# Layer 2's attention: one PSUM copy on ScalarE, one block of row sums earlier, and another order of work on GpSimd

## The reference, cut to what matters

```python
xn = layernorm(x, g1)
q = xn @ Wq.T                                   # 16 heads of 64
k, v = split(xn @ Wkv.T)                        # one head of 64 each
q, k = l2norm(q * 16) * 4, l2norm(k) * 4
sim = where(causal, q @ k.T, -max)
attn = softmax(sim)
out = layernorm((attn @ v) @ Wout.T, g2)
x = x + out + (silu(xn @ w_gate) * (xn @ w_up)) @ w_down
```

## Time and profile before

| | before |
|---|---|
| median of 3 runs | 1240.59 (1240.56 to 1241.66) |
| the profiled execution's own time | 1239.02 |
| its span, first to last instruction | 1237.2 |
| granted PE clock, mean over the span | 0.98 |
| busy: PE | 1145.6 (93%) |
| busy: DVE | 921.7 (74%) |
| busy: ACT | 672.3 (54%) |
| busy: POOL | 490.6 (40%) |

### The profile page before, as it was taken

The page is one execution under the profiler, slowest core; times in us unless marked ns, Lnnn a source line. Parts: engine busy times, 40 slices in busy tenths (PEclk is TensorE's granted clock), DMA queues, the critical chain, the costliest instruction groups (busy, mean ns, idle before and its releaser), DMA issues.

```text
span 1237.2 us, 26393 instructions
## 1 busy us (share of the span) xinstructions
PE 1145.6 (93%) x8475; PEld 782.4 (63%) x8475; DVE 921.7 (74%) x2473; ACT 672.3 (54%) x1290; POOL 490.6 (40%) x691
## 2 busy tenths in 40 slices
PE   5999999999999998899399999999999999999996
PEld 3656666666666554799265857657576575765764
DVE  7888888888888897455456868668686686866755
ACT  2767676666676755355173552735527355273550
POOL 5122212121222311554364481744817448274450
PEclk8999999999999998899799999999999999999999
DMA  3311212020101000122011030210302103021020
GB/s 89 101 44 48 56 28 57 26 60 26 33 18 27 18 18 1 44 64 55 15 35 27 9 59 0 42 25 8 59 0 42 25 8 59 0 49 19 15 46 10
DMA packets 43718, 42.31 MB, mean 34 GB/s; under 512 B 7040, under 2 KB 36224, under 8 KB 43648
## 3 DMA queue, kind: packets, MB, share of 16 engines
q0 software_dynamic: 11008, 17.31, 8.0%
q1 hardware_dynamic: 32640, 24.15, 7.3%
HBM read 13.72 MB, written 6.75 MB: 17 GB/s over the span
## 4 chain that ended last, share of the span: by engine, by line
issue 19%; PE 11%; POOL 9%; DVE 7%; DMA 3%; ACT 1%; POOLq 0%; DVEq 0%; ACTq 0%
PE pair L496 4%; POOL q_len L1272 3%; DMA arena<-arena 3%; PE gather L496 2%; PE ring_d L496 2%; POOL arena L1231 2%; POOL arena L1313 2%; PE ring_a L496 1%; PE pair L500 1%; DVE q_len L1958 1%; DVE stats L1574 1%; POOL arena L1293 1%; DVE arena L2106 1%; DVE q_rn L1960 1%; ACT arena L1515 1%
## 5 line engine op out<-in xcount | busy, mean ns | idle before, releaser
L1378 ACT ACTIVATE arena<-ring_a 128x384 f32<-128x384 f32 (+1 forms) x512 | 253.6, 550 | 147.1 <-PE ring_a L496 146.9
L1126 POOL TENSOR_SCALAR_AFFINE_SELECT arena<-arena 128x512 f32<-128x512 f32 x128 | 82.4, 643 | 366.6 <-ACT arena L1378 366.4
L496 PE MATMUL ring_a<-q_max,rows 128*128 128x384 f32 (+1 forms) x512 | 197.2, 388 | 2.2 <-DVE q_max L1684 1.8
L1670 DVE CUSTOM_DVE_ANT_0 arena<-pair,arena 128x384 bf16<-128x384 f32 (+1 forms) x269 | 161.3, 614 | 23.6 <-PE pair L496 19.1
L1272 POOL TENSOR_TENSOR q_len<-q_sum,exponents 128x8 f32<-128x8 f32 x64 | 113.6, 1775 | 85.1 <-DVE q_sum L2000 85.1
L1535 ACT ACTIVATE arena<-ring_a 128x1024 f32<-128x1024 f32 x96 | 99.1, 1032 | 75.9 <-PE ring_a L496 75.7
L496 PE MATMUL ring_a<-q_parts,k_rows 64*128 64x384 f32 (+2 forms) x1152 | 128.3, 344 | 3.4 <-ACT q_parts L1523 2.4
L496 PE MATMUL ring_a<-arena,v_aug 128*32 128x384 f32 (+1 forms) x1024 | 123.5, 553 | 1.7 <-POOL arena L1126 0.6
L496 PE MATMUL pair<-arena,v_aug 128*64 128x512 f32 (+3 forms) x768 | 114.0, 439 | 3.4 <-ACT arena L1535 3.0
L496 PE MATMUL pair<-rows,q_rows 128*128 128x384 f32 (+1 forms) x269 | 110.0, 411 | 3.3 <-DMA rows<-k_rows 2.5
L496 PEld LDWEIGHTS ring_a<-q_max,rows 128*128 128x128 f32 x512 | 96.8, 191 | 21.4 <-ACT arena L1378 5.3
(11 more groups left out here) (275 smaller groups left out, 2380.9 us busy)
## 6 DMA issues: line engine op xcount, KB each, us to landing
arena<-arena POOLq DMA_DIRECT2D x32, 384.0 KB, 4.6
rows<-k_rows SPq DMA_DIRECT2D x128, 64.0 KB, 2.0
arena<-in_w SPq DMA_DIRECT2D x16, 256.0 KB, 2.8
slots_y<-arena SPq DMA_DIRECT2D x39, 64.0 KB
x_all<-in_x SPq DMA_DIRECT2D x8, 256.0 KB, 3.8
tokens_x<-xn SPq DMA_DIRECT2D x8, 256.0 KB, 2.7
out<-o_t SPq DMA_DIRECT2D x8, 256.0 KB, 2.3
arena<-tokens_x,tokens_now POOLq DMA_INDIRECT x40
```

Source lines behind the costliest of these rows:

```text
L496: return pe.matmul(out, lhs, rhs, start=start, stop=stop, skip_group_check=True)
L1126: pool.affine_select(out=v, in_=v, compare_op=ALU.is_ge, fill=0.0, base=0, pattern=[[0, HG], [1 if late else -1, P]], channel_multiplier=- ...
L1378: act.activation(probs[:, t % NT, h, 0:many], A.slot(("cols", c))[:, 0:many], ACT.Exp).then_inc(A.free.sem, A.free.add(1))
L1670: dve.tensor_tensor_reduce(dump[:, h % 2, 0:many], M.slot(("max", n))[:, 0:many], masks[:, m, at:at + many], 1.0, LOWEST, ALU.add, ALU.max ...
```

## The change

- ScalarE, not VectorE, copies the values of pair 5 out of PSUM; it does so at the end of its work for n = 6. VectorE counts the copy as done in its bookkeeping (`O.free.add(1)`) and goes from `q_low(7)` straight to `add_blocks(5)`.
- `sums1(2)` moves from behind `values1(6)` to the place directly behind `scores(7)`. `sums1(1)` stays where it was.
- GpSimd's order for each n becomes: power, masks, gathers, folds. The four gathers are split one, two, one over n = 0, 1, 2 (before: none, two, two).
- `fold(0)` is issued behind the masks and the gather of n = 2, `fold(1)` behind the masks of n = 3, `fold(2)` and `fold(3)` both behind the masks of n = 4 and ahead of `both_roots`. Before, they were issued at the head of n = 2, 3, 4 and 5.
- A fold no longer waits for the one before it. Folds 0 and 1 count on one semaphore and folds 2 and 3 on another, and `sums1(m)` waits until its own has both.

```diff
--- before.py
+++ after.py
@@ -99,7 +99,7 @@
 PER_C = dict(squared=6, q_full=6, q_free=6, o_full=7, o_free=7, l_full=1, l_free=1, s_full=15, s_free=15, m_full=8, m_free=8, w_full=11, w_free=11,
              e_full=10, e_free=9, own=17, var=1, veps=1, rstd=1,
              sums=6, lens=6, q_lo=8, h1=3, masked=24, pv=4, added4=6, g_free=2, inverted=1, fin=1, stored=16,
-             folded=16 * N_FOLD)
+             folded0=32, folded1=32)
 
 CREDITED = dict(q_lo=1, q_free=1, o_free=1, l_free=1, s_free=1, m_free=1, w_free=1, e_free=1, g_free=1, sums=1, h1=1, r_free=1, added=1, stored=1, pv=1,
                 xt_free=1, y_full=1, y_free=1, staged=2, out0=1, out1=1, out2=1, out3=1)
@@ -872,7 +872,7 @@
                     if m == 0:
                         pe.wait_ge(s["g_free"].sem, s["g_free"].at(b, 0))
                     if m < N_FOLD // 2:
-                        pe.wait_ge(s["folded"].sem, s["folded"].at(b, 32 * (m + 1)))
+                        pe.wait_ge(s[f"folded{m}"].sem, s[f"folded{m}"].at(b, 32))
                     if m == 2:
                         pe.wait_ge(s["added4"].sem, s["added4"].at(b, 6))
                     for j in ((0, 2, 3), (0, 2, 3), (0,), range(NT))[m]:
@@ -890,8 +890,8 @@
                     scores(n)
                     if n + 2 < NP:
                         project_q(n + 2)
-                    if n == 6:
-                        sums1(1)
+                    if n > 5:
+                        sums1(n - 5)
                     if n + 1 < NP:
                         turn_q(n + 1)
                     if n + 1 < HC:
@@ -900,8 +900,6 @@
                         values1(n - 1)
                     if n == 5:
                         sums1(0)
-                    if n == 7:
-                        sums1(2)
                 values1(NP - 1)
                 if not last:
                     turn_x(b + 1)
@@ -1287,16 +1285,14 @@
                 def fold(n):
 
                     pool.wait_ge(s["o_full"].sem, s["O"].filled(b, ("o", n)))
-                    if n:
-                        pool.wait_ge(s["folded"].sem, s["folded"].at(b, 16 * n))
+                    folded = s[f"folded{n // 2}"]
                     apart(pool)
                     pool.dma_start(probs_of(n, 0)[:, :, P:T], probs_of(n, 1),
-                                   accum_op=ALU.add).then_inc(s["folded"].sem, s["folded"].add(16))
-
-                s["folded"].restart()
+                                   accum_op=ALU.add).then_inc(folded.sem, folded.add(16))
+
+                for name in ("folded0", "folded1"):
+                    s[name].restart()
                 for n in range(NP):
-                    if 0 <= n - 2 < N_FOLD:
-                        fold(n - 2)
                     if n + 2 < NP:
                         q_length(s, n + 1, b)
                     p = probs1[n % PB]
@@ -1315,8 +1311,10 @@
                         ins.then_inc(s["masked"].sem, s["masked"].add(1))
                     if not last and n == 0:
                         fetch_slots(b + 1)
-                    if not last and n in (1, 2):
-                        fetch(b + 1, (2 * n - 2, 2 * n - 1))
+                    if not last and n < 3:
+                        fetch(b + 1, ((0,), (1, 2), (3,))[n])
+                    for of in {2: (0,), 3: (1,), 4: (2, 3)}.get(n, ()):
+                        fold(of)
                     if not last and n == 4:
                         both_roots(b + 1)
                 if not last:
@@ -1494,7 +1492,7 @@
 
             def attend(b, last):
                 s = SC
-                Q, S, M, W = (s[k] for k in "QSMW")
+                Q, O, S, M, W = (s[k] for k in "QOSMW")
                 for name in ("s_free", "m_free", "w_free", "squared"):
                     s[name].restart()
 
@@ -1544,6 +1542,9 @@
                         q_turned(n + 1)
                     if n + 1 < HC:
                         gate_up(n + 1)
+                    if n == 6:
+                        act.wait_ge(O.full.sem, O.filled(b, ("o", 5)))
+                        act.activation(o1[:, 5, :], O.slot(("o", 5))[:], ACT.Copy).then_inc(O.free.sem, 1)
                 if not last:
                     move_x(b + 1)
                     move_kv(b + 1)
@@ -2072,9 +2073,10 @@
                     if n + 1 < NP:
                         dve.wait_ge(S.free.sem, S.emptied(b, ("q.T", n + 1)))
                         q_low(n + 1)
-                    if n:
+                    if n and n != 6:
                         values_out(n - 1)
                     if n == 6:
+                        O.free.add(1)
                         add_blocks(5)
                     if n + 2 < NP:
                         q_unit(s, n + 2, b)
```

## The result

The kernel after takes 1225.82 us (median of 4 runs, 1222.92 to 1228.28) against 1241.12 for the kernel before beside it (1240.56 to 1242.59): a ratio of 0.987, 95% interval 0.9849 to 0.9892. The forecast was 1226.4. The profiled execution took 1224.63 with a span of 1222.9, that is 14.4 and 14.3 us less than before.

A forecast was written before the change was run, and what follows sets the result against it. PE works 72.76 of 77.00 us per loop pass, so only its gaps can be won: 7 x (1.24 + 0.50 + 0.20) + 0.45 + 0.20 = 14.2 off 1239.02 gives 1224.8, or 1226.4 against the median; range 1222.9 to 1236.

The forecast's parts named there:

- the three named: PE's waits per pass: 1.5 us before pair 6's projection, 0.5 before the row sums, 0.4 before a product of values.
- Gathers and fold 0: One gather fewer ahead of pair 5's power, so pair 6's projection starts earlier: gain 1.24 us a pass, bounds 0.94 and 1.50.
- the power ends 1.71 later: On GpSimd, pair 5's power ends 1.71 us behind fold 0's end, at 800.05 instead of 801.29.
- The 2.29 of rows 4: Length in us shown for pair 5's power before, beside 1.64 of another; read from the fold's end it is 1.71.
- The gather at n = 0: The gather moved there fits into 2.01 us in which POOL waits for DVE, 0.44 left: priced at nothing.
- Folds 2 and 3: Issued together behind pair 4's masks, removing the DMA wait before the sums: gain 0.50 us a pass, 0.95 in the first.
- Copy and early sums: ScalarE's copy and sums1(2) ahead of values1(6): PE's idle falls from 0.41 to 0.2, gain 0.2 us in all eight passes.
- The slower rival: POOL can't issue fold 3 until fold 2 has landed; PE loses 0.7 us a pass against before: 1245.5, chance 0.08.
- The 1233: Time near which the slower case would end if a fold landed in 2.9 us by the Trainium skill's rule.
- DVE binds: Rival: DVE's chain to pair 7's low parts keeps its place, losing the sums' gain at pair 7's scores: 1231.9, chance 0.14.
- the power stays late: Rival: power and fold slow each other again, or one gather takes two's time; only sums' gains remain: 1235.0, chance 0.10.
- No effect: Rival: PE's gaps open elsewhere, each wait gone being taken up by the next one: 1240.6, chance 0.06.

The follow-up runs named there:

- The reduction: Kernel after, with the floor on query lengths made by a maximum over pairs instead of multiply-and-maximum with two constants: ratio 0.9754, pass 73.5 us.
- the folds alone: Kernel after with copy back on VectorE, sums back behind pair 6's values, gathers none, two, two; only folds moved and unchained: ratio 1.0021.
- Forced: Kernel after, but GpSimd waits for fold 0 to land before issuing fold 1, and for fold 2 before fold 3: ratio 1.0065, pass 78.4 us.
- GpSimd's order alone: Kernel after with the copy back on VectorE and sums of pairs 4 and 5 back behind pair 6's values: ratio 0.9909, pass 75.4 us.

## Why the prediction was right, point by point

The time fell as forecast, 14.4 us in the profiled execution against 14.2. Which waits of PE would shrink was right. That the sum came out so closely was luck: several terms were off, and the errors made up for each other, within a pass and outside it. PE's starts in the pass of the rows above, against the same stretches of before:

| stretch on PE | before | after | gain | forecast |
|---|---|---|---|---|
| projection of pair 5 to that of pair 6 | 7.52 | 6.90 | 0.62 | 1.24 |
| to that of pair 7 | 6.15 | 5.95 | 0.20 | 0 |
| from there to the scores of pair 6 | 5.48 | 5.47 | 0.01 | 0 |
| to the scores of pair 7 | 7.22 | 6.66 | 0.56 | 0.50 |
| to the end of pair 7's values | 8.36 | 7.84 | 0.52 | 0.20 |

- **What bounds.** Right: the gain came from PE's waits, the three named and a fourth before the projection of pair 7.
- **Gathers and fold 0.** Half the price. The fold stood 1.33 behind the gather's start, where 1.39 was worked out from its row. The step that failed was "the power ends 1.71 later": it ended 2.19 later. The floor behind it, whose cost I had left in the 1.63 between power and PE, grew from 0.49 to 0.74. The reduction shows that the floor's length depends on how it is written; that the subtraction holds the power is argued from the rows. The 2.29 of rows 4 was no warning, as there the fold alone explains it. A row that would have warned is the same power in the last loop pass of before, whose subtraction starts 0.03 behind the fold's end and which ends 2.23 behind that end:

```profile
1106.54 2.42 POOL L1272 TENSOR_TENSOR q_len<-q_sum,exponents 128x8 f32<-128x8 f32 x1
```

- **The gather at n = 0.** Right: it is hidden.
- **The projection of pair 7** was priced at nothing and won 0.20: the floor of pair 6 fell from 0.49 to 0.16, probably as its phase against the masks changed.
- **Folds 2 and 3.** Right, 0.56 for 0.50. Both were issued in 2.41, the power for pair 7 came earlier, and no wait for a DMA is left. Fold 3 was issued at 804.54 and landed 6.0 later, 1.1 before PE wanted it at 811.61; the forecast had 1.0 to spare. With the folds alone the term is there too, but the clock takes it back.
- **Copy and early sums.** 0.52 for 0.20. I had counted 0.2 of idle before the sums, with additions of 2.27; they took 2.14 and no idle was left. PE starts the sums 2.31 behind the scores' start, where it had started the values after 2.69. Another 0.14, priced at nothing, comes from the order, as sums and both products run 5.53 instead of 5.67.
- **The slower rival.** Its mechanism does not occur: GpSimd issues fold 3 without waiting. Forced, it costs 1.4 a pass against before, where I had 0.7. The 1233 given there for a quicker landing has no sum behind it. "DVE binds" and "the power stays late" did not come either, though the second was half right. "No effect" came in one part only, the folds alone, and there by the clock.
- **Outside these passes.** The last loop pass won 3.2 instead of 1.9: only there does the power for pair 5 end 1.71 behind the fold, as the forecast had it for every pass, and the wait before the projection of pair 6 is gone. The last pass won 0.6 for 0.2, but the tail gave 0.9 back, which I had not foreseen. And 1.0 of the 14.3 was there before phase C began.

## What to carry to other kernels

A tiny instruction on a chain between engines is priced by what its neighbour is doing, not by its size: look at the spread of its durations (shortest, median, longest) before moving work around it. When one of them is held in steps of another engine's instructions, change its form first; here that was worth 1.65 a pass on top of the reordering's 1.85. Edits on one chain may overlap: split a sum of terms into runs before believing any one of them. And where a run shows no gain, look at the granted clock of its passes before calling the edit worthless.

## What the runs showed of the hardware

- A VectorE multiply-and-maximum by constants on 128x8 elements in place took 158 to 1435 ns in the kernel before, beside GpSimd's masks; a reduction that gives the same values took 157 to 171.
- Behind a wait of 2.0 us the granted PE clock fell in five of seven passes with the folds alone, and a projection of eight matmuls took 1.77 instead of 1.16 us; behind the 1.5 of before it fell in none.
- GpSimd issues two accumulating DMAs of 384 KB within 2.41 us and doesn't wait for the first; one issue is mostly recorded with 1.2 to 1.4 us.
- In the tail, PE stands idle for 1.90 us while VectorE takes the reciprocal and what follows it, in both kernels. Behind that the granted PE clock differs by run. The windows of the kernel after and then of before (window, length, busy PE, PEld, DVE, ACT, POOL, PE clock, DMA share, GB/s):

```profile
1205.00:1211.00 6.00, 5.74 (x31) 5.24 (x32) 3.22 (x6) 0.00 (x0) 0.00 (x0) 0.72 0.00 0
```

```profile
1220.00:1226.00 6.00, 5.74 (x44) 5.18 (x43) 4.34 (x8) 0.00 (x0) 0.00 (x0) 1.00 0.01 3
```

At 0.72 PE spent part of the window at the lower level of 1.2 GHz. The tail took 23.3 us after and 22.4 before; in the runs it lay between 21.6 and 24.0. It was 24.0 with GpSimd's order alone, where the clock fell the same way. From the reciprocal to PE's last matmul it is 16.2 after and 14.6 before; the final store, from its issue to the end of the span, is 0.7 shorter after. The lower clock in this stretch is why the last pass's gain didn't arrive.
